# Graph and LSTM kernel: four products of the o gate issued behind the low products of i and g

## The reference

```python
i_t = sigmoid(xi_t + h @ V_i)
g_t = tanh(xg_t + h @ V_c)
o_t = sigmoid(xo_t + h @ V_o)
c_new = h * c + i_t * g_t
h_new = o_t * tanh(c_new)
```

## Time and profile before

| | |
|---|---|
| median of 3 runs | 520.42 us (519.90 to 520.51) |
| span of the profiled execution, first to last instruction | 520.4 us |
| PE busy | 428.4 us |
| DVE busy | 371.6 us |
| ACT busy | 358.8 us |
| matmuls of L1205 | 3096 in 361.1 to 507.3 us |

### The profile page before, as it was taken

The page is one execution under the profiler, slowest core; times in us unless marked ns, Lnnn a source line. Parts: engine busy times, 40 slices in busy tenths (PEclk is TensorE's granted clock), DMA queues, the critical chain, the costliest instruction groups (busy, mean ns, idle before and its releaser), DMA issues.

```text
span 520.4 us, 15606 instructions
## 1 busy us (share of the span) xinstructions
PE 428.4 (82%) x6160; PEld 372.2 (72%) x6160; DVE 371.6 (71%) x1195; ACT 358.8 (69%) x931; POOL 176.9 (34%) x322
## 2 busy tenths in 40 slices
PE   2476899978899999999999999956777778888880
PEld 2254677867788888888888888845767667777770
DVE  2776999987887768668677335353677778888883
ACT  0342698456776677677767745567799989999980
POOL 4443500254444446446445334201222222222220
PEclk9996799999999999999999999986599999999996
DMA  3334000330000001000000010010000000100111
GB/s 117 138 105 123 1 2 31 104 104 15 28 24 1 1 15 38 1 3 29 23 3 1 13 39 1 2 50 1 3 3 3 4 3 4 52 25 31 54 52 55
DMA packets 9293, 16.92 MB, mean 33 GB/s; under 512 B 1694, under 2 KB 7139, under 8 KB 9214
## 3 DMA queue, kind: packets, MB, share of 16 engines
q1 hardware_dynamic: 7658, 13.32, 7.6%
q10 hardware_dynamic: 676, 1.67, 0.8%
q0 software_dynamic: 880, 0.86, 0.7%
HBM read 6.23 MB, written 9.61 MB: 30 GB/s over the span
## 4 chain that ended last, share of the span: by engine, by line
PE 38%; DVE 29%; ACT 11%; issue 8%; POOL 7%; DMA 5%; DVEq 0%; SPq 0%; ACTq 0%; POOLq 0%
PE bank L1128 10%; PE bank L1205 7%; PE bank L1097 7%; PE bank L1099 6%; DVE hots L1465 6%; DMA x_sb<-in_x_dram 5%; ACT tc L921 4%; DVE h L1660 3%; DVE h L1704 3%; PE bank L1051 3%; ACT gate L907 3%; DVE c_st L1655 3%; POOL rstd L634 2%; PE bank L1145 2%; POOL newton L633 2%
## 5 line engine op out<-in xcount | busy, mean ns | idle before, releaser
L1205 PE MATMUL bank<-h,V 128*128 128x63 f16 (+1 forms) x3096 | 109.9, 195 | 28.4 <-DVE h L1660 25.2
L1205 PEld LDWEIGHTS bank<-h,V 128*128 128x128 f16 x3096 | 101.3, 99 | 40.2 <-issue 33.6
L1051 PE MATMUL bank<-hots 128*128 128x125 f16 x625 | 120.8, 223 | 0.0
L1465 DVE TENSOR_TENSOR hots<-iota,kp 128x1024 f16<-128x1024 f16 x157 | 105.6, 698 | 19.9 <-PE bank L1051 16.9
L1097 PE MATMUL bank<-h_flat,counts 125*128 125x257 f16 x375 | 97.3, 273 | 0.4 <-ACT counts L776 0.4
L1099 PE MATMUL bank<-h_flat,counts 125*128 125x256 f16 x375 | 96.4, 271 | 0.0
L633 POOL TENSOR_SCALAR newton<-rstd,var_eps 125x1 f32<-125x1 f32 x48 | 33.3, 694 | 119.8 <-DVE rstd L1537 117.4
L776 ACT ACTIVATE counts<-bank 125x500 f16<-125x500 f32 x96 | 55.2, 607 | 20.6 <-PE bank L1051 19.1
L665 POOL TENSOR_TENSOR hc<-h_flat,c_st 128x126 f32<-128x126 f32 x82 | 35.0, 426 | 101.0 <-DVE c_st L1655 99.0
L1097 PE MATMUL bank<-h_flat,gx 125*128 125x257 f16 x250 | 68.2, 274 | 0.0
L1099 PE MATMUL bank<-h_flat,gx 125*128 125x256 f16 x250 | 67.4, 270 | 0.0
(11 more groups left out here) (168 smaller groups left out, 814.6 us busy)
## 6 DMA issues: line engine op xcount, KB each, us to landing
h_dram<-h_flat SPq DMA_DIRECT2D x1, 3137.2 KB
x_dram<-x_sb SPq DMA_DIRECT2D x5, 625.0 KB
out_dram<-x_sb SPq DMA_DIRECT2D x4, 625.0 KB
x_sb<-in_x_dram SPq DMA_DIRECT2D x3, 625.0 KB
x_sb<-in_x_dram ACTq DMA_DIRECT2D x2, 625.0 KB
out_dram<-x_sb SPq DMA_DIRECT2D x1, 375.0 KB
gx<-in_L_gnn_weight_dram ACTq DMA_DIRECT2D x1, 256.0 KB, 4.2
gx<-in_L_ffn_U_i_dram SPq DMA_DIRECT2D x1, 256.0 KB, 2.7
```

Of the source, the lines that this page charges most:

```text
L1051: nc.tensor.matmul(ps_count[group % 3][:, pos * KEYS:(pos + 1) * KEYS], hots[:, ring, 0, g // 2, :, g % 2], hots[:, ring, 1, g // 2, 0:KEY ...
L1205: mm = nc.tensor.matmul(to[:, (m - m0) * n:(m - m0 + 1) * n], V16[:, v_part, d, m * P:(m + 1) * P], h16[:, h_part, d, c0:c1], start=False, ...
L1465: nc.vector.tensor_tensor(hots[:, k % RING, :, :, :, :].rearrange("p a h n g -> p (a h) n g"), iota[:, :, :].unsqueeze(1).to_broadcast(of) ...
```

## The change

In full_products, the four o products of the low part of V with the high part of h move from ahead of the wait on lo_ready[q] to behind the eight products of i and g with the low part of h. The numbers of products, their operands and banks and the semaphores stay as they are; the o products of (high, high) stay ahead of the wait. full_products is called for the 84 halves of turns 29 to 70 (and in the general path).

```diff
             def full_products(q, turn, hi_seen, lo_seen):
                 pe.wait_ge(ig_seed[q], turn)
                 pe.wait_ge(hi_ready[q], hi_seen)
                 for part in PRODUCTS[:2]:
                     multiply(q, 0, 2 * HH, ps_g[q], part, False)
                 pe.wait_ge(o_seed[q], turn)
-                for part in PRODUCTS[:2]:
-                    multiply(q, 2 * HH, MT, ps_x[q], part, False)
+                multiply(q, 2 * HH, MT, ps_x[q], PRODUCTS[0], False)
 
                 pe.wait_ge(lo_ready[q], lo_seen)
                 multiply(q, 0, 2 * HH, ps_g[q], PRODUCTS[2], True).then_inc(ig_ps[q], 1)
+                multiply(q, 2 * HH, MT, ps_x[q], PRODUCTS[1], False)
                 multiply(q, 2 * HH, MT, ps_x[q], PRODUCTS[2], True).then_inc(o_ps[q], 1)
```

## The result

| | before | after |
|---|---|---|
| median of 5 runs | 520.46 us (519.90 to 521.83) | 517.40 us (516.82 to 518.04) |
| span of the profiled execution | 520.4 us | 515.0 us |
| its own time | | 516.82 us |

The ratio is 0.9933, with a 95% interval of 0.9914 to 0.9951: 3 us, 0.7% less. Measured again on another chip, the changed kernel took 518.10 beside 521.25 for the kernel before, again 0.9937 (0.9920 to 0.9953). The forecast was 516.5 with a range of 515.6 to 518.4. Of the 23 runs of the kernel before on that second chip one took 2230.07 us; it counts as slow, is left out of every ratio, and its cause is not known.

A forecast was written before the change was run, and what follows sets the result against it. Loops of waits, not a full engine, bound the kernel: turns fall from 3.22 to 3.12 us, 40 turns from 130.04 to 126.31 with hiccups; 3.73 plus 0.20 at turn 30 saves 3.9, giving 516.5 us, range 515.6 to 518.4.

The forecast's parts named there:

- Loop A: A half round its own turn, PE start to gate, tc and next PE start: 3.22 us per turn, falling to 3.10.
- Loop C: From gate to gate through the low part and its eight products on PE: 1.56 us per half, 3.12 per turn.
- the hiccups: Irregular turns such as turn 50, and the end of the round: 1.24 us in 40 turns before, 1.51 after.
- Half 1: ... nothing gained, the gate is where it was.: Half 1 of turn 48: PE reaches the low wait at 435.48 and stands until 435.60, no gain.
- The wait costs 0.06 and no restart: PE at the low wait: first low product 0.06 us behind the low part, not 0.14 as at a half's head.
- Rival 3: PE restarts at the low wait, 0.14 us instead of 0.06: turn 3.28, some 523.0 us; chance 0.06.
- The cover of o_ps: At L915 on ACT: o_ps eight instead of four products behind ig_ps, 0.24 us instead of 0.12; 0.17 of cover remains.
- loop B: From gate to gate through c: gate to tc 1.29 us, tc to next gate 0.27, at most 1.56 per half.
- Turn 29 to 30: First full turns at half clock: four products of 0.05 us bring turn 30's gate 0.20 sooner, at 375.61.
- Rival 1: Gain partly given back as late halves can't catch up: turn 3.14 to 3.16 us, time 517.7; chance 0.13.
- Rivals 2 and 4: Full turns: no gain, turn stays 3.22, 520.3 us, chance 0.05; or PE falls to half clock, 545 us, chance 0.01.
- The execution's own time: Whole profiled execution: 520.4 us, taken as level with the median of runs, 520.42, becomes 516.5.

## Why the prediction was right, step by step

*Loop A holds the kernel before, at 3.22, and falls by 0.0294 per product.* Right, and shown from both sides: 28, 24 and 22 products ahead give 3.336, 3.220, 3.162.

*What is late next is the low part, in both halves.* Right: with 20 and with 16 products the same 3.13, and 2.984 once nothing waits for it.

*Loop C is 3.12.* It is 3.129. In half 0 the way from the first low product to the gate is 0.451 instead of 0.441 (means over the turns), so its half is 1.567 and not 1.56. The earlier trace rows had shown it already: 0.51 from low part to gate in half 0, where the sum takes 0.50 for both halves. In 40 turns that is 0.36, nearly all of what lacks in the 40 turns: 3.73 forecast, 3.32 and 3.37 found. The other 0.05 is in the hiccups, 1.56 instead of 1.51.

*"Half 1: ... nothing gained, the gate is where it was."* True of the single turn that I looked at and wrong as a statement on the part. Half 1's share of the edit is needed: without it its own loop holds the turn at 3.204. The sum wasn't harmed, because it went by the loops and not by the halves. A sign fell with it: the 36 matmuls of half 1 were to take 1.3 and more, and take 1.26 (mean 1.25). The stall of 0.12 kept half 1's PE start where it was; by the loops only the turn less loop A is left, 3.13 - 3.10 = 0.03. Where the start does stay, with half 1 alone moved and the turn at 3.22, they take 1.34.

*The wait costs 0.06 and no restart.* Right: the first low product is 0.06 behind the low part in every full half of the kernel after, from turn 30 on, with a stall of 0.01 as with one of 0.28. Rival 3 is out.

*The cover of o_ps.* Right in kind, L915 stays 0.37 behind L907, but the 0.17 left is too much: it is 0.13. The 0.04 from the last awaited product to ACT was added for L907 and not for L915, which has the same way to go: with 16 products behind ig_ps both start 0.23 behind the start of the product that they wait for. 0.37 less 8 x 0.0294 is 0.13, and with eight products more L915 was 0.10 late, as 0.235 - 0.13 asks. That each 0.01 beyond the cover goes into loop B is wrong too: those 0.10 cost nothing.

*Turn 29 to 30.* Not shown either way. Forecast 3.77; 3.78 in the second profile of the changed kernel, 3.44 in the first. In the first the granted clock was 0.93 in 372 to 377; in the second it was 0.50 in 372 to 374 and 0.82 in 374 to 377, so PE came to the 2.4 GHz level later there. Over the eleven profiles of the changed kernel and of the experiments it goes from 3.33, with half 0 issued as in the kernel before, to 3.87. So the 0.20 of the sum can't be told from the clock.

*Rival 1, partly given back.* It asks for 3.14 to 3.16 per turn and 517.7. The time, 517.40, lies nearer to it than to 516.5 and could not have told; the turn of 3.129 and 3.128 does, as it repeats within 0.002. Loop B, which that rival needs at 3.12, can go down to 2.98 (no low wait). Rivals 2 and 4 fall by the turn and by a clock of 1.00 behind 377.

*The hiccups.* Right in kind (turn 50: gates 435.52 and 437.35, so 1.83 behind the one before, 0.26 more than a usual 1.57).

*The execution's own time.* Wrong. I set the span of 520.4 level with the median of 520.42. Beside it the kernel after has 516.82 for a span of 515.0, so 1.8 lies around the span, and by my estimate from that the profiled execution of before was one of about 522.2. The sum came to no harm, because the saving was taken off the median too. The saving of 3.9 that was forecast stands against 3.06 and 3.15 between medians on one chip each, and 3.32 and 3.37 in the 40 turns. What the median of the kernel before moved from one chip to another (520.46, 521.25, 521.69, 520.91) is of the size of what is left, so that rest was not followed further. The two intervals hold a saving of 2.5 to 4.5 and of 2.5 to 4.2, so the times alone don't refute 3.9.

*Small slips.* Forecast and rival 1 add up to 0.88 and not 0.89, and slower is 0.07 with rival 4. It is c and not ig that needs hc; c is later, so the slack is larger than the 0.48.

## What to carry to other kernels

Where two halves of a tile hand each other the engines, add up every loop: each half round itself, and from one to the other. An edit that shortens a loop in one half alone can give nothing although the timeline shows one slow half only; the slack changes sides. And where a chain of waits and a second path are level, the chain may name only one of them: here, taking the other away told.

Work that only a later consumer needs belongs behind the wait that an urgent consumer stands at. Here it cost nothing up to that later consumer's slack, and 0.10 us beyond it.

A price taken from one operation on an engine holds beside the neighbours that it was measured with. The low part on POOL was a fair 0.40 alone and 0.54 beside the DVE operations that the change put it next to.

## What had not been expected of the hardware

An f32-less-f16 subtraction of 128x124 or 128x126 took 0.541 us on POOL in the steady turns, with DVE's ig and c beside it, and 0.40 with no DVE operation beside it. On DVE it took 0.282. DVE's c grew from 0.282 to 0.384 beside it.
